# A Macaron block with a Mamba scan: one of the four dt·x·B tiles moves to GpSimd, and one projection moves ahead

## What is computed

```python
x_proj = x @ W_x.T
dt_x, Bm, Cm = jnp.split(x_proj, [R, R + N], axis=-1)      # R = 64, N = 16 states
dt = jax.nn.softplus(dt_x @ W_dt.T + b_dt)
A = -jnp.exp(A_log)
dA = jnp.exp(jnp.einsum('bld,dn->bldn', dt, A))
dBx = jnp.einsum('bld,bln,bld->bldn', dt, Bm, x)
...
h = dA_t * h + dBx_t                                       # over the 512 tokens
y_t = jnp.einsum('bdn,bn->bd', h, C_t)
y = ys.swapaxes(0, 1) + x * D
```

## Time and profile before

| | before |
|---|---|
| median of 3 runs | 437.2 us |
| profiled execution | 437.5 us, span 435.8 us |
| TensorE busy | 399.7 us (92%) |
| VectorE busy | 326.9 us (75%) |
| ScalarE busy | 275.1 us (63%) |
| GpSimd busy | 271.7 us (62%) |
| granted TensorE clock | 0.999 |
| scan stage, first to last scan | 142.15 to 325.53 us |

### The profile page before, as it was taken

The page is one execution under the profiler, slowest core; times in us unless marked ns, Lnnn a source line. Parts: engine busy times, 40 slices in busy tenths (PEclk is TensorE's granted clock), DMA queues, the critical chain, the costliest instruction groups (busy, mean ns, idle before and its releaser), DMA issues. The chain is left out here.

```text
span 435.8 us, 8330 instructions
## 1 busy us (share of the span) xinstructions
PE 399.7 (92%) x2716; PEld 277.1 (64%) x2716; DVE 326.9 (75%) x510; ACT 275.1 (63%) x512; POOL 271.7 (62%) x212
## 2 busy tenths in 40 slices
PE   6899899899996898899899999898999899899995
PEld 5347444444354778788898799888984556344452
DVE  5687565554388989999899999989886865456552
ACT  1430465564148789789999999998952210656553
POOL 7204356653328489998979798969881006577543
PEclk9999999999999999999999999999999999999999
DMA  8968115842604234465445458442310524334411
GB/s 262 385 193 249 49 55 171 276 174 110 204 6 97 74 91 147 104 135 144 141 108 126 149 123 131 120 148 93 121 54 0 197 95 115 95 119 136 118 54 49
DMA packets 50809, 56.85 MB, mean 130 GB/s; under 512 B 16327, under 2 KB 35596, under 8 KB 50768
## 3 DMA queue, kind: packets, MB, share of 16 engines
q1 hardware_dynamic: 46624, 45.78, 35.9%
q0 software_dynamic: 4144, 10.54, 8.2%
HBM read 41.14 MB, written 16.48 MB: 132 GB/s over the span
## 5 line engine op out<-in xcount | busy, mean ns | idle before, releaser
L526 POOL TENSOR_TENSOR gs<-hs,c_sb 128x1024 f32<-128x1024 f32 x63 | 148.2, 2374 | 23.8 <-PE bank L1056 13.1
L1425 DVE TENSOR_TENSOR_SCAN hs<-da,bank 128x1024 f32<-128x1024 f32 x64 | 143.7, 2272 | 4.5 <-PE bank L1039 2.3
L664 ACT ACTIVATE da<-dt_sb,a_neg 128x511 f32<-128x511 f32 x128 | 84.2, 710 | 2.9 <-DVE hs L1425 1.5
L1056 PE MATMUL bank<-ident,gs 128*128 128x128 f32 x504 | 65.7, 274 | 4.8 <-POOL gs L526 3.2
L680 ACT ACTIVATE dbx_t<-dtx_t,h_sb 128x256 f32<-128x256 f32 x153 | 65.2, 495 | 1.7 <-DVE dtx_t L1394 1.6
L1056 PEld LDWEIGHTS bank<-ident,gs 128*128 128x128 f32 x504 | 56.6, 141 | 7.6 <-POOL gs L526 5.1
L881 PE MATMUL bank<-xnT,w_gu 128*128 128x512 f32 x112 | 50.2, 595 | 0.0
L480 POOL DMA_INDIRECT da<-rows,row_token x29 | 30.6, 1057 | 29.8 <-issue 29.4
L1032 PE MATMUL bank<-ident,dbx_t 128*128 128x128 f32 x336 | 44.2, 275 | 5.3 <-DVE dbx_t L1409 1.8
L592 ACT ACTIVATE th<-bank,da 128x256 f32<-128x256 f32 x36 | 17.0, 473 | 43.1 <-PE bank L920 30.4
L1032 PEld LDWEIGHTS bank<-ident,dbx_t 128*128 128x128 f32 x336 | 37.4, 141 | 9.7 <-issue 6.0
(11 more groups left out here) (184 smaller groups left out, 772.9 us busy)
## 6 DMA issues: line engine op xcount, KB each, us to landing
c_sb<-c_dram SPq DMA_DIRECT2D x64, 256.0 KB, 3.3
rows<-xn_no SPq DMA_DIRECT2D x8, 516.0 KB, 5.3
diag_dram<-dbx_t SPq DMA_DIRECT2D x6, 512.0 KB
routing<-diag_dram SPq DMA_DIRECT2D x11, 256.0 KB, 3.5
slot_m<-diag_dram SPq DMA_DIRECT2D x11, 256.0 KB, 3.4
rows<-xn_no SPq DMA_DIRECT2D x1, 2064.0 KB, 9.6
x_sb<-in_x SPq DMA_DIRECT2D x4, 512.0 KB, 5.8
w_gu<-in_gate_w SPq DMA_DIRECT2D x2, 1024.0 KB, 9.9
```

The source lines that it names most:

```text
L526: nc.gpsimd.tensor_tensor(gs[:, s % 2], hs[:, s % RING], c_sb[:, s % RING].unsqueeze(1).to_broadcast([P, KC, L]), ALU.mult).then_inc(sc_g, 1)
L664: nc.scalar.activation(da[:, s % RING, k, 1:L], dt_sb[:, k, seq(s // N)][:, 1:L], ACT.Exp, scale=a_neg[:, k, s % N:s % N + 1]).then_inc(sc ...
L1056: mm = nc.tensor.matmul(YA[k][:, i * P:(i + 1) * P], products[:, k, i * P:(i + 1) * P], ident[:], start=(s % N == 0 and i == 0), stop=(s % ...
L1425: nc.vector.tensor_tensor_scan(hs[:, s % RING].rearrange(flat), da[:, s % RING].rearrange(flat), DBX[s % 2][:, :, :].rearrange(flat), 0.0, ...
```

## The change

In batches 1, 2 and 3 VectorE makes no dt·x·B tile any more. GpSimd makes the last of the four tiles of the states n = 0, 1, 3, 10, 12 and 14 in batches 1 and 2, and of n = 8, 10, 11, 12 and 14 in batch 3: 17 tiles of 128x256. ScalarE makes three tiles of these states; it did so already for n = 0, 1 and 3, and made four of the others. So VectorE loses 6 tiles, ScalarE 11. The tile of state s+4 stands behind product s in GpSimd's queue, except that those of a batch's first two states stand together behind product n = 13 of the batch before. TensorE's turn waits for GpSimd's tile as well. On TensorE, the projection of batch 1 stands ahead of addition 0 and not behind it.

```diff
--- before.py
+++ after.py
@@ -49,7 +49,8 @@
     RING = 4
     TURNS = 3
     STATES = BATCH * N
-    BY_DVE = ((2, 2, 2, 1, 1, 1) + (0,) * 10,) + ((1, 1, 0, 1) + (0,) * 12,) * 2 + ((0,) * 16,)
+    BY_DVE = ((2, 2, 2, 1, 1, 1) + (0,) * 10,) + ((0,) * 16,) * 3
+    BY_POOL = ((0,) * 16,) + ((1, 1, 0, 1) + (0,) * 6 + (1, 0, 1, 0, 1, 0),) * 2 + ((0,) * 8 + (1, 0, 1, 1, 1, 0, 1, 0),)
     DIAG = ((6, 7, 9, 10, 12, 14),) + ((4, 6, 7, 9, 11, 13),) * 2 + ((4, 7, 9, 13),)
     BLOCKS = 6
     DIAGS = 2
@@ -234,8 +235,8 @@
         diag_b = [sem(f"diag_b{j}") for j in range(BLOCKS)]
         diag_in = [sem(f"diag_in{u}") for u in range(DIAGS)]
         c_in = [sem(f"c_in{u}") for u in range(RING)]
-        sc_da, sc_act, sc_dve, sc_dbx, sc_h, sc_g, sc_tp, sc_x = (
-            sem(f"sc_{s}") for s in ("da", "act", "dve", "dbx", "h", "g", "tp", "x"))
+        sc_da, sc_act, sc_dve, sc_pool, sc_dbx, sc_h, sc_g, sc_tp, sc_x = (
+            sem(f"sc_{s}") for s in ("da", "act", "dve", "pool", "dbx", "h", "g", "tp", "x"))
         sc_last = sem("sc_last")
 
         def pj_bank(b, k):
@@ -268,7 +269,8 @@
 
         def states_by(engine, s):
 
-            return sum({"dve": BY_DVE[t // N][t % N] > 0, "act": BY_DVE[t // N][t % N] < LT}[engine] for t in PLAIN if t < s)
+            return sum({"dve": BY_DVE[t // N][t % N] > 0, "pool": BY_POOL[t // N][t % N] > 0,
+                        "act": BY_DVE[t // N][t % N] < LT}[engine] for t in PLAIN if t < s)
 
         def plain_buffer(s):
 
@@ -514,6 +516,17 @@
                 tiles = slice(LT * b, LT * (b + 1))
                 nc.gpsimd.tensor_tensor(x_sb[:, tiles], xn[:, tiles], x_sb[:, tiles], ALU.add).then_inc(back_x, 1)
 
+            def tile(s):
+
+                b, n = divmod(s, N)
+                if s not in PLAIN or BY_POOL[b][n] == 0:
+                    return
+                pool.wait_ge(sc_dbx, turned_before(s))
+                pool.wait_ge(pj_btc, b + 1)
+                pool.wait_ge(pj_dtx, 2 * (b + 1))
+                nc.gpsimd.tensor_tensor(plain_buffer(s)[:, LT - 1, :], dtx_t[:, b % 2, LT - 1, :],
+                                        b_t[:, b, LT - 1, n:n + 1].to_broadcast([P, D]), ALU.mult).then_inc(sc_pool, 1)
+
             def scan(b):
                 for n in range(N):
                     s = N * b + n
@@ -525,6 +538,11 @@
                         pool.wait_ge(sc_tp, s - 1)
                     nc.gpsimd.tensor_tensor(gs[:, s % 2], hs[:, s % RING], c_sb[:, s % RING].unsqueeze(1).to_broadcast([P, KC, L]),
                                             ALU.mult).then_inc(sc_g, 1)
+                    if n == N - 3:
+                        if s + 3 < STATES:
+                            tile(s + 3)
+                    if n != N - 4 and s + 4 < STATES:
+                        tile(s + 4)
                     if b == 0 and n == 3:
                         combine(BATCH - 1)
                     if b == 0 and n == 5:
@@ -667,7 +685,7 @@
             def outer(s):
 
                 b, n = divmod(s, N)
-                mine = LT - BY_DVE[b][n]
+                mine = LT - BY_DVE[b][n] - BY_POOL[b][n]
                 if s not in PLAIN or mine == 0:
                     return
                 if s == 0:
@@ -1027,6 +1045,7 @@
                 if s in PLAIN:
                     pe.wait_ge(sc_act, states_by("act", s + 1))
                     pe.wait_ge(sc_dve, states_by("dve", s + 1))
+                    pe.wait_ge(sc_pool, states_by("pool", s + 1))
                     for k in range(KC):
                         for i in range(LT):
                             mm = nc.tensor.transpose(DBX[s % 2][:, k, i * P:(i + 1) * P], plain_buffer(s)[:, i, k * P:(k + 1) * P], ident[:])
@@ -1080,12 +1099,12 @@
                         ln_transposes(1, 5)
                     if last_one(s):
                         shared_gate_up(1, 1, 0, (0,))
+                    if s == 1:
+                        project(1)
                     if n > 0:
                         add(s - 1)
                     if not more and n in PIECES:
                         shared_piece(PIECES.index(n))
-                    if s == 1:
-                        project(1)
                     late = (2, 1, 0, 0)[b]
                     if more and n in (late, late + 1):
                         project_z(b + 1, n - late)
```

## The result

| | before | changed |
|---|---|---|
| median, first comparison (14 executions each) | 438.08 us | 440.88 us |
| ratio, 95% interval | | 1.0067 (1.0050 to 1.0084) |
| profiled execution, span | 435.8 us | 437.8 us |
| VectorE busy | 326.9 us | 325.0 us |
| ScalarE busy | 275.1 us | 271.0 us |

The changed kernel is slower by 0.67%, 2.9 us on 437.2, or 440.1 us. The spans, given to 0.1 us, differ by 2.0 us: 0.33 us lie ahead of the first scan, where nothing was changed, and 1.76 us between the first scan and the last add_y; behind it the two profiles agree to 0.03 us.

A forecast was written before the change was run, and what follows sets the result against it. Four engines run in step, and the loop that matters runs through GpSimd, whose products TensorE's additions wait for. The terms 0.0 + 1.1 + 0.2 + 1.2 = +2.5 us on 437.2 gave 439.7 us, range 436.9 to 443.0.

The forecast's parts named there:

- The tile's price: GpSimd's time for one 128x256 tile: 0.74 us, 0.70 us of its queue, with bounds of 0.20 and 1.22 us.
- Step 1: Batch 0: the projection fits into TensorE's 1.58 us wait ahead of addition 0; product 13 ends 1.5 us sooner.
- Step 2: Tiles 16 and 17 behind product 13: turn 17 comes as before, the 1.5 us are gone, 0.0 us in all.
- Step 3: End of batch 1: tiles 30, 32 and 33 delay GpSimd's products, so addition 31 and add_y come later; +1.1 us.
- Step 4: End of batch 2: tiles 42, 44 and 46 delay product 47, partly offset at ScalarE's table load; +0.2 us.
- Step 5: Batch 3: tiles 56, 58, 59, 60 and 62 delay products that additions 53 and 62 wait for; +1.2 us.
- (b): Rival: a tile costs up to 1.22 us, nearly every tile in later steps adds 0.5 us; about +8, 445; chance 0.12.
- (c): Rival: the head's gain lasts, with a tile below 0.35 us; about -0.6 us, 436.6 us; chance 0.14.

The follow-up runs named there:

- the dummies: Six more dummy matmuls on TensorE in its wait ahead of turn 0: added to the changed kernel 1.0057, to the kernel with only the projection moved 0.9968.

## Why the prediction was right, step by step

**The tile's price** was the term furthest off, and only in size: 0.615 us, not 0.74 (start to start 0.57 to 0.59, not 0.70). The line between the 4-column and the 1,024-column row was too steep for this instruction. By the rule of the Trainium skill, "GPSIMD Engine Reference", Engine selection, which the prediction cites, the tile came to 0.80 us, an estimate; it took 0.615 us, 1.5 times VectorE's 0.402 us and not twice.

**Step 1** (1.5 us won in batch 0): shown, 1.62 us by the profile, and by the projection alone, which keeps it.

**Step 2** (all of it lost at tile 16): shown by the wait of 1.71 us at turn 16, and from the other side: scan 17 is 1.5 us sooner with the first states back on VectorE. Left after the two: -0.12 us instead of 0.0.

**Step 3** (+1.1 us at the end of batch 1): +0.79 from scan 17 to add_y 1. The mechanism is as worked out (product 30, addition 30, projection, addition 31); with the dearer tile the sum had 0.3 us too much. That VectorE's removed tiles pay nothing is shown for tiles 32 and 33; for the other four it is argued.

**Step 4** (+0.2 us): 0.09 us. ScalarE's table load waits for the piece, as said.

**Step 5** (+1.2 us): 1.00 us by the profile, and shown by taking the tiles out, which leaves it at 0.

The steps sum to +1.8 us where 2.5 were forecast, and all of them have the sign and the place given. The timed ratios say 2.3 to 2.9 us. The forecast of 439.7 us lies 0.4 us under the 440.1 of the first comparison, and that closeness is in part luck: a sum 0.7 us too high, mostly by the tile's price, stood in for time that the profile doesn't show and the prediction didn't have. **What that time is was not settled**, but the record points at one cause that the prediction left out. It took TensorE's 1.58 us ahead of addition 0 for free room, and the profiles with a fall show that it was a reserve: filled, it no longer takes up a fall of the clock at the head of the scan (above). Between executions at a mean clock of 0.989 or more the difference is 1.8 to 1.9 us, the profile's; at 0.988 or less it is 3.3 us, 1.5 more, near the 1.58 us of the reserve. Against it as the whole account: the kernels with only the projection moved have filled the same wait, and their timed gain is 0.9 to 1.5 us, only 0.1 to 0.7 under the profile's 1.6. Nor does any run show that the change makes falls more frequent: 2 of 22 executions of the changed kernel were at 0.997 or more, against 21 of 100 of the kernel before, which is too few to tell, and the dummies didn't change the ratio.

**The rivals.** (b), a tile of 1.22 us at about +8 us, didn't happen, but two tiles each came to 1.046 us and +6.5 (profile) to +7.7 us (timed), which bears out that the loss grows with the price. (c) would have needed a tile under 0.35 us. Its other half, that the head's gain lasts, is true without the tiles of the first states: the kernel that has them back on VectorE keeps 1.5 us up to batch 3.

## What to carry to other kernels

Idle time of an engine is not room for work: GpSimd had 23.8 us of it, the tiles took 10.4, and 3.3 us came out at the end, because they stood in the few places where its product is what the next engine waits for. Before work is put on an engine, look in the timeline for who waits behind that place in its queue, and by how little; six tiles cost 2.3 us with the states that open a batch and six others 0.1 us with its later states. The same holds for a wait that a move fills: here it had also taken up falls of the clock. Test the two halves of a change apart: here one alone is 0.2 to 0.3% faster than the kernel before, and the other hid it.

## What the runs showed of the hardware

A GpSimd multiplication with a broadcast scalar from a tensor took 0.615 us for 128x256 and 1.046 us for 128x512, so 0.43 us for each further 256 columns, while the product, whose second input is a full row of 512 used for both chunks, takes 2.374 us for 1,024, and a tensor_scalar of 128x256 with per-partition scalars 1.223 us, twice the tile's time. In all profiles the mean product took 2.37 to 2.38 us, tiles or not.

A fall of TensorE's clock to its lower level for some 7 us (by the two windows of 0.50 and 0.83) around the first scan cost four profiles 2.1 to 2.2 us, all of it carried to the end, as much as the change that was measured; all four have the projection moved. A shorter one (0.66 in a window of 5 us) cost 1.1 us in a kernel with the projection moved and nothing in one without, where a wait of 1.58 us shrank to 0.37.
